# A 12-layer perceiver in float32 on one core: one key projection unit in every pair step, the first half of the scores behind one bank of transposes, key copies in column halves, expert weights in full tiles and five value units computed in an earlier layer

## What is computed

```
L0x: x += xn @ W1.T + mean(ctx, rows) @ W2.T + b                # all of ctx is read once
L0a: x += gated linear attention, 16 heads of 16, causal
L0f: x += sum over the 2 best of 8 experts: (silu(xn@W1_e) * (xn@W2_e)) @ W3_e   # hidden width 704
L2x: q = xn@Wq+bq; k = ctx@Wk+bk; v = ctx@Wv+bv                 # ctx: 12544 keys
     x += softmax(mask(q k' / 4)) v @ Wo + bo                   # 16 heads of 16
L3x: the same with other weights, no biases, an additive mask
L3f: 2 of 8 experts, tokens dispatched to slots, hidden width 1024
```

## Time and profile before

| what | us |
|---|---|
| median of 3 runs | 1661.11 (1659.79 to 1663.58) |
| the profiled execution | 1664.46, its span 1662.7 |
| L0f, from its first projection to its last product | 78 to 155 |
| L2x, from its first K unit to its last `multiply` | 344 to 895 |
| L3x, the same | 1002 to 1570 |
| L3f | 1590 to 1660 |

### The profile page before, as it was taken

How to read it: one execution, slowest core, us unless ns; L and a number is a source line. 1 busy time by engine, 2 the same in 40 slices (tenths; PEclk the granted TensorE clock), 3 DMA queues, 4 the chain that set the end, 5 groups by cost and what they waited for, 6 DMA issues and landing times.

```text
span 1662.7 us, 34203 instructions
## 1 busy us (share of the span) xinstructions
PE 1544.9 (93%) x14044; PEld 1147.0 (69%) x14044; DVE 1028.4 (62%) x1933; ACT 918.0 (55%) x1371; POOL 9.7 (1%) x22
## 2 busy tenths in 40 slices
PE   6999998988999999999987998899999999997897
PEld 5777587756677777777766675677777777775663
DVE  5522323656777787777775325677777777777631
ACT  3021032127777777777774222677777777778610
POOL 0000000000000000000000000000000000000000
PEclk9999999899999999999999999999999999999999
DMA  9667854245434243434322364543424243324445
GB/s 394 221 199 237 312 193 197 80 171 186 153 142 169 90 169 110 149 112 168 115 87 109 129 244 166 179 155 118 156 89 156 90 156 108 139 89 166 161 170 206
DMA packets 39533, 267.67 MB, mean 161 GB/s; under 512 B 4760, under 2 KB 5016, under 8 KB 32152
## 3 DMA queue, kind: packets, MB, share of 16 engines
q1 hardware_dynamic: 39384, 265.55, 44.0%
HBM read 159.49 MB, written 3.28 MB: 98 GB/s over the span
## 4 chain that ended last, share of the span: by engine, by line
PE 77%; ACT 7%; DMA 6%; DVE 5%; issue 3%; SPq 1%; POOL 0%; DVEq 0%; ACTq 0%; POOLq 0%
PE T L786 14%; PE O L808 8%; PE S L772 8%; PE O L786 7%; PE T L744 7%; PE T L757 5%; PE S L648 4%; ACT sc L1199 4%; PE O L744 3%; PE O L942 3%; PE T L643 3%; PE S L1094 3%; PE O L1123 3%; PE O L757 2%; DMA keys<-keys_hl 2%
## 5 line engine op out<-in xcount | busy, mean ns | idle before, releaser
L1612 DVE CUSTOM_DVE_ANT_0 sc<-S,mask_bias,small 128x896 f32<-128x896 f32 x336 | 377.7, 1149 | 62.7 <-PE S L772 56.7
L1199 ACT ACTIVATE sc<-sc,small 128x1792 f32<-128x1792 f32 x168 | 299.8, 1786 | 2.3 <-DVE small L1612 1.0
L1185 ACT ACTIVATE pT<-T 128x512 f32<-128x512 f32 x378 | 220.2, 594 | 123.1 <-PE T L786 119.4
L786 PE MATMUL T<-consts,sc 128*128 128x128 f32 x1592 | 239.6, 281 | 6.8 <-ACT sc L1199 2.2
L786 PEld LDWEIGHTS T<-consts,sc 128*128 128x128 f32 x1592 | 176.1, 141 | 72.9 <-issue 38.2
L808 PE MATMUL O<-pT,arena 128*32 128x128 f32 x6272 | 198.4, 278 | 28.8 <-ACT pT L1185 28.8
L808 PEld LDWEIGHTS O<-pT,arena 128*32 128x32 f32 x6272 | 169.4, 111 | 67.9 <-issue 66.6
L772 PE MATMUL S<-keys,q 64*128 64x512 f32 (+1 forms) x896 | 150.8, 414 | 15.5 <-DVE small L1612 14.3
L1578 DVE COPY pT<-T 128x512 f32<-128x512 f32 x150 | 99.9, 686 | 100.1 <-PE T L786 100.0
L1185 ACT ACTIVATE pT<-O 128x512 f32<-128x512 f32 x182 | 108.1, 594 | 56.0 <-PE O L786 54.9
L1612 DVE CUSTOM_DVE_ANT_0 packs<-S,mask_bias,small 128x896 f32<-128x896 f32 x112 | 128.5, 1147 | 0.0
(11 more groups left out here) (355 smaller groups left out, 1905.8 us busy)
## 6 DMA issues: line engine op xcount, KB each, us to landing
keys<-keys_hl SPq DMA_DIRECT2D x112, 896.0 KB, 7.9
ctx_in<-in_ctx_cols SPq DMA_DIRECT2D x46, 896.0 KB, 7.0
wide<-in_ctx_rows SPq DMA_DIRECT2D x14, 896.0 KB, 4.7
wide<-in_up_L0f SPq DMA_DIRECT2D x8, 1408.0 KB, 9.7
sc<-in_ctx_cols SPq DMA_DIRECT2D x10, 896.0 KB, 5.7
wide<-in_up_L2f SPq DMA_DIRECT2D x8, 1024.0 KB, 6.6
wide<-in_down_L2f SPq DMA_DIRECT2D x8, 1024.0 KB, 4.9
wide<-in_up_L3f SPq DMA_DIRECT2D x4, 2048.0 KB, 9.0
```

Source lines behind the costliest of these rows:

```text
L786: last = nc.tensor.transpose(ring(plan, u)[:, t * P:(t + 1) * P], weights_of(2 * m + i)[:, b * P:(b + 1) * P], ident)
L1185: nc.scalar.activation(pT2[:, g * BANK:(g + 1) * BANK], ring(plan, u), ACT.Copy).then_inc(s["t_act"], 1)
L1199: nc.scalar.activation(weights_of(n), weights_of(n), ACT.Exp, bias=n_best[c % 2][:, h:h + 1], scale=-1.0, accum_out=l_new[c % 2][:, h:h + ...
L1612: V.tensor_tensor_reduce(weights_of(n)[:, i * HC:(i + 1) * HC], S4f[:, n % 2 * 2 * BANK:n % 2 * 2 * BANK + HC], mask_bias[:, i * HC:(i + 1 ...
```

## The change

1. **Order of a pair step.** S0 now stands behind T0 alone instead of behind T2. The V unit stands between T2 and T3. Exactly one K unit stands just before `multiply` in each step that projects (m < 48), so the table is replaced by `KEY_STEPS` and `VALUE_STEPS`; L2x has its five V units in steps 0, 2, 3, 4 and 6, L3x its seven in steps 0 to 6.
2. **Who empties what.** DVE empties T0 and T4, ACT T1, T2, T3, T5, T6 and the V units. ACT's K part stands between the two exponentials, DVE's is its last work on a step's scores. The quad reduction of DVE stands between the two second-half passes.
3. **Key copies in column halves.** Each copy of a feature half is issued as two groups of four DMAs of half the columns, with a semaphore each.
4. **Values of chunk 4 made whole in L0x and L0a.** Five more value units (`AFTER`) are computed in place of `warm` matmuls of L0a. L2x then has no V unit in the steps of chunk 3. The write to DRAM waits for them, and SP's loads of the first expert weights of L0f stand behind that write.
5. **L0f in full tiles.** The 704 columns are cut in five tiles of 128 and one of 64 instead of eight of 88.
6. **L3f loads.** Both pairs of `up` loads stand ahead of both pairs of `down` loads; one `warm` run is 14 instead of 20.

```diff
-KEPT = {"L2x": 2, "L3x": 0}
-PROJECTED = {
-    "L2x": {0: [("V", 2)], 1: [("K", 0, 0), ("V", 3)], 2: [("K", 0, 1), ("K", 0, 2)], 3: [("K", 0, 3), ("V", 4)],
...
+WHOLE = 4
+KEPT = {"L2x": [0 if c == 1 else 7 if c == WHOLE else 2 for c in range(7)], "L3x": [0] * 7}
+KEY_STEPS = [(hf, nb) for hf in range(KD) for nb in range(KEY_UNITS)]
+VALUE_STEPS = {"L2x": {0: 2, 2: 3, 3: 4, 4: 5, 6: 6}, "L3x": {j: j for j in range(VALUE_UNITS)}}
...
 def emptied_by(u):
-    return "act" if u[0] == "T" and u[2] not in (0, 1) else "dve"
+    return "act" if u[0] == "V" or u[0] == "T" and u[2] not in (0, 4) else "dve"
...
@@ SyncE, the key copies @@
-                    def load_keys(c, hf):
+                    def load_keys(c, hf, half):
 
-                        sp.wait_ge(s["t_dve"], plan.emptied(("K", c, hf, KEY_UNITS - 1)))
+                        sp.wait_ge(s["t_dve"], plan.emptied(("K", c, hf, 2 * half + 1)))
                         if c:
 
-                            sp.wait_ge(s["s_ready"], 2 * (NP * (c - 1) + NP // 2 * (hf + 1)))
+                            sp.wait_ge(s["s_ready"], 2 * (NP * (c - 1) + NP // 2 * (hf + 1) - 1) + half + 1)
+                        part = slice(half * HC, (half + 1) * HC)
...
@@ SyncE, L3f @@
+                    load_ups(2)
+                    load_ups(3)
+                    load_downs(2)
+                    load_downs(3)
...
@@ TensorE, L0a @@
+                if layer == "L0a":
+                    after(2, T2[:, 1])
+                    after(3, O2[:, 1])
+                    after(4, S4[:, 3], 2)
...
-                    qkv(layer, x2T, 25)
+                    qkv(layer, x2T, 1)
...
@@ TensorE, the pair step @@
                 for m in range(PAIRS):
-                    for g in range(3):
-                        turn(m, g)
+                    turn(m, 0)
                     if m + 1 < PAIRS:
                         scores(m + 1, 0)
-                    turn(m, 3)
-                    project(m, 0)
-                    turn(m, 4)
-                    turn(m, 5)
+                    turn(m, 1)
+                    turn(m, 2)
+                    if plan.values_of(m):
+                        value_unit(*plan.values_of(m)[1:])
+                    for g in range(3, 6):
+                        turn(m, g)
                     if m + 1 < PAIRS:
                         scores(m + 1, 1)
                     turn(m, TURNS - 1)
                     if quad_turned(m) is not None:
                         turn_quad(quad_turned(m))
-                    project(m, 1)
+                    if plan.keys_of(m):
+                        key_unit(*plan.keys_of(m)[1:])
                     multiply(m)
...
@@ TensorE, L0f @@
-                    for t in range(E):
-                        last = mm(O2[:, b, 0:D], hidT[0:F // E, t, :], w[:, t, :], start=(t == 0), stop=(t == E - 1))
+                    for t, rows in tiles(layer):
+                        last = mm(O2[:, b, 0:D], hidT[0:rows, t, :], w[0:rows, t, :], start=(t == 0),
+                                  stop=(t == tiles(layer)[-1][0]))
...
@@ ScalarE, the pair step @@
                 for m in range(PAIRS):
+                    take_turned(m, 1)
                     take_turned(m, 2)
                     if quad_turned(m) is not None:
                         take_quad(quad_turned(m))
-                    take_turned(m, 3)
-                    project(m, 0)
-                    for g in range(4, TURNS):
+                    if plan.values_of(m):
+                        value_unit(*plan.values_of(m)[1:])
+                    for g in (3, 5, 6):
                         take_turned(m, g)
                     if m + 1 < PAIRS:
                         soften(2 * m + 2)
-                    project(m, 1)
+                    if plan.keys_of(m):
+                        key_unit(*plan.keys_of(m)[1:])
                     if m + 1 < PAIRS:
                         soften(2 * m + 3)
...
@@ VectorE, the pair step @@
                     take_turned(m, 0)
-                    take_turned(m, 1)
                     if m + 1 < PAIRS:
                         for n in range(2):
                             take_scores(2 * m + 2 + n, 0)
-                    project(m, 0)
+                    take_turned(m, 4)
                     if m + 1 < PAIRS:
-                        for n in range(2):
-                            take_scores(2 * m + 2 + n, 1)
+                        take_scores(2 * m + 2, 1)
                     if quad_turned(m) is not None:
                         take_quad(quad_turned(m))
-                    project(m, 1)
+                    if m + 1 < PAIRS:
+                        take_scores(2 * m + 3, 1)
+                    if plan.keys_of(m):
+                        key_unit(*plan.keys_of(m)[1:])
```

More of the change, by code:

```diff
@@ L46, with tiles @@
 GATED = ("L0f", "L3f")
+def tiles(layer):
+    return [(f // P, min(P, FF[layer] - f)) for f in range(0, FF[layer], P)]
 PACKS = {
@@ L957, in expert @@
                     for j in range(2):
-                        last = transposes(T2[:, j], hid[:, j * F // 2:(j + 1) * F // 2], 4, F // E)
+                        for t, rows in tiles(layer)[4 * j:4 * j + 4]:
+                            last = nc.tensor.transpose(T2[0:rows, j, t % 4 * P:(t % 4 + 1) * P],
+                                                       hid[:, t * P:t * P + rows], ident)
                         last.then_inc(s["t_ready"], 1)
@@ L1220, in cross @@
                     key_unit(0, 0, nb)
+                for b in plan.values:
+                    value_unit(0, b)
                 for n in range(2):
```

207 lines of the change are left out of this document (122 added, 85 removed), and 4 rows, old and new, of the table PROJECTED.

## The result

The changed kernel takes 1601.1 us (median of 4 runs, 1600.68 to 1609.01) against 1662.34 us (4 runs, 1659.79 to 1664.24) for the kernel before on the same chip: a ratio of 0.9644, 95% interval 0.9611 to 0.9677. The forecast was 1605.0, range 1586 to 1621, faster with 0.94. The profiled execution took 1601.17; its span of 1599.4 is 63.3 us shorter than before's.

What follows compares the result with a forecast made beforehand. It took TensorE, 77% of the chain that ended last, as the bound. Terms summed to 56.3 us off the profiled 1664.46, giving 1608.2; the runs' median lies 3.35 lower, so 1604.8, forecast as 1605, range 1586 to 1621.

Steps and rivals of the forecast that it cites:

- signs of being wrong: K-alone steps over 8.3 us, scores waiting for VectorE in over 25 places, or TensorE waiting for weights from L0a to L0f.
- V units: Chunk 3 of L2x: five units leave its steps at 1.73 us each, free in L0a; 8.7 us gained.
- Weight loads busy for 55 of 76 us: L2x: a rival view that TensorE is not the bound and removed matmuls return as waits; 1623 us, 6%.
- Last chunks: L2x and L3x steps without projection: earlier S0 takes two banks, 0.98 us, out of the loop; 9.8 us gained.
- Waits ahead of `multiply`: Projecting steps of the cross layers: a K unit covers the emptying of T6; 26 us gained.
- first chunks: L2x and L3x: key copies by halves arrive in time, and score waits go with S0 ahead; 8.3 us gained.
- what is given back: Cross layers: the K-part loop slightly exceeds TensorE's work, and mask and sums no longer hide; 13.8 us lost.
- mask: VectorE work in step 6 that delays step 7 by 0.7 us in 12 chunks; 8.4 us lost.
- sums: Four short operations adding up the last chunk in step 0 delay step 1 of L2x five times; 3.5 us lost.
- Key copies: Cross layers: 224 DMAs of 448 KB replace 112 of 896 KB and land in time; cost 0.
- L0f: Eight experts: four second-product instructions and two transposes fewer save 1.15 us each, if weights come in time; 9.2 us gained.
- L3f: Fourth pair's up weights issued earlier: 5.34 us of wait and 2.8 of low clock go; 8.1 us gained.

Runs made afterwards that it cites:

- experiment 10: Kernel before with only the load of L0f's down weights changed, to 128 partitions (1024 KB for 704 KB on 88): 1659.29 us, ratio 0.9982.
- experiment 11: Kernel before with only L3f's load order changed, fourth pair's up weights directly behind the third's, all down weights behind both: 1656.02 us, ratio 0.9956.
- experiments 6 to 9: Changed kernel with mask in halves, 1600.22 us; sums moved to step 2, 1601.95; both, 1599.94; mask, sums beside V units and alpha's difference moved, 1598.43.

## Why the prediction was right, step by step

The time, the sign and the list of what the trace would show came out: 16 waits ahead of `multiply`, K alone 7.97 us (7.9), step 7 8.69 (8.6), K with V and quad 10.09 (10.1), last chunk 7.45 (7.4), no wait in L3f, an expert at 8.3 (8). One of its signs of being wrong did show, though small: TensorE waits once for up weights of L0f, 0.5 us. Of the 63.3 us the sum had 56.3. The terms:

- *V units* 8.7, measured 8.4. Weight loads busy for 55 of 76 us were no sign of room.
- *Last chunks* 9.8, measured 7.4, of which 1.5 is the step at low clock; against experiment 10 it is 5.9. A step gained 0.86 where 0.98 was set: what goes is S1's wait of 0.87, not the two banks of 0.98. It gained it in six steps of L2x, not seven, and in L3x two steps gained 0.6 each, not three 0.98.
- *Waits ahead of `multiply`, first chunks, and what is given back*: 26 + 8.3 - 1.9 - 11.9 = 20.5, measured 30.3 (18.8 + 4.0 + 7.5), and 24.1 against experiment 10 (14.8 + 1.8 + 7.5). Most of what is missing is a term of *First chunks* that the prediction put at nothing and did count in L3f: the low clock behind the waits. In experiment 11, where it lasted 6.8 us from 387.0, steps 1 and 2 of chunk 0 take 23.55 us in L2x, in the kernel before with 3.4 us 21.90, and 20.78 in experiment 10, with 3.4 us ahead of the wait and none behind it. Where the other 3.6 us come from was not traced.
- *What is given back*: mask 8.4, measured (8.69 - 7.97) x 6 + (8.54 - 7.97) x 6 = 7.7; sums 3.5, measured 0.64 x 5 = 3.2. Right in place and size. The four attempts to get it back (experiments 6 to 9) gave 1.7 to 4.4 us of step time.
- *Key copies* 0. Right for the halves, since no wait is left. But the step did not see that the halves are what the order stands on: without them the kernel is 90 us slower than before. That belonged among the rivals.
- *L0f* 9.2, measured 7.8. An expert saves 0.74 us of TensorE's work, not 1.15: from start to start sixteen instructions take 3.46 us, not the 3.62 of the earlier trace rows, and twelve take 2.78, more than 12/16 of it. That is 5.9; 2.3 came from the load, which had no term, and 0.5 went to one wait. Two errors nearly cancel.
- *L3f* 8.1, measured 8.0.

The cross layers together were forecast at 39.0 us and measured at 38.3 with the clock of experiment 10. That this is so close is partly luck: the last chunks were set 3.9 too high and the waits 3.6 too low.

The prediction added up moves as if each had its own worth. The experiments show that they have not: K and V in the new places with the old score half are worth 0.6 us or less, the early score half with K in the middle leaves the kernel 4.3% slower than before, the early half in the old order 1.1% slower, and together they save 33.7 us of step time beside the V units (28.2 against experiment 10). The 26 us of the second term are thus not K's alone. What the other parts of the order give by themselves (ACT emptying the V units, the quad between the passes) was not tried. What the sum got right is the length of the new step, worked out as the longer of TensorE's work and the loop, and that is why the total held.

## What to carry to other kernels

Cut a step at the two hand-overs of its loop and compare TensorE's work in each stretch with the chain that runs beside it: here 3.85 us from S1 to the next T0. A unit that feeds nobody soon belongs in the stretch that has room, and its worth is read from the new length of the step, not from the waits that its place had. When a producer is spread evenly over the steps, ask what each transfer now has for time: here a group of copies that took 13.8 us from issue to landing stood one step of 10 us ahead of the next writer of its source, and had to be cut into parts. Before a difference is put down to the order, hold the granted clock of the two stretches against each other.

## What the runs showed of the hardware

- A load of 1024 KB on 128 partitions let the 1408 KB behind it land after 7.7 us, where one of 704 KB on 88 partitions led to 9.7.
- Copies of half the size between two tiles on the core land after 4.5 us instead of 7.9.
- TensorE's granted clock falls for stretches of 3.4 or 6.8 us, also in steps whose code is the same as in steps without one. The part from the last `multiply` of L3x on, almost to the end, had no such stretch in two kernels and lasted 85.8 us; with 3.4 us at 1.2 GHz it lasted 87.0 to 87.1 in five, with 6.8 us 88.7 in three. A step of 8.31 us with 3.4 of it at 1.2 GHz took 9.78.
- Lengths of a step at full clock repeat within some 0.02 us, even between kernels, while whole executions differ by 3 us and more outside them; a gain of 4 us that the steps show is lost in the interval of the ratio.
